# A chunk more ahead of each seven-product down-projection, and the third step of the weight sums by an accumulating DMA

## The chip, the cores and the metric

The kernel runs on one core of a Trainium2 chip, in one launch. The metric is the time of an execution on the device in microseconds (us), the median of several runs. PE is TensorE, DVE VectorE, ACT ScalarE, POOL GpSimd, SP SyncE.

## The reference

Two layers on x of 1024 tokens (8 x 128) and 512 features, all in float32.

```
y  = x W^T + 2 * gated low-rank of 8 experts (top 2)     # _L0_cond_ref
x  = x + series(y) + silu(y Wg^T) * (y Wu^T) Wd^T        # _L0_attn_ref; the FFN has 1248 hidden
z  = x W2^T + b + 2 * LoRA of the sequence's adapter     # _L0_cond2_ref
x  = x + FFN with LoRA (1376 hidden)                     # _L0_ffn_ref
```

The change is in the FFN of the second line (the "first FFN"): 1248 hidden features are padded to 10 chunks of 128.

## The kernel before, in words

Activations lie with features on the partitions. A product in float32 is made as three matmuls of fp32r parts: each operand is split into a high part (ACT copies it, `copy`, L481) and a low part (DVE subtracts, `lo`, L922); low x high, high x low and high x high are summed in PSUM. A matmul here is 128x128 weights on 512 columns.

The first FFN is a series of 14 blocks, `BLOCKS` (L79). A block ("u", c) makes gate and up of chunk c for both halves of the tokens, a block ("d", n) makes a quarter of a down-projection over four chunks. Each is a 2x2 block product made with seven products in place of eight (`seven1`): p1 to p7, each 6 matmuls, 42 per block. The operands of an up block are made once (HT: B11, B21, B22, T1 to T4). Those of a down block are made of the gated chunks: each pair of chunks (even, odd) gives B11 and T1 from the even one, then T2, T3, then B21, B22, then T4 from the odd one, all split, in G. Chunks 8 and 9 (`TAIL`) are not in a down block: they are multiplied in the ordinary way at the end (`tail`, 48 matmuls).

Weights of a block come as two pieces of [128, 512] (`P_BLOCK[q]`, `P_BLOCK[q] + 1`), loaded by SP into a ring of four slots of `raw`, and as `parts`, from which four sums of weights (S1 to S4) are made in three steps: SP loads 1024 columns (L436), POOL adds 768 columns by an accumulating DMA (L462), DVE adds the third summand of two of them (`sums1`, L1089). A region for sums is shared by blocks of one parity. ACT then splits the small part (256 columns, `part1_hi1`) and the large part (1536 columns, `part2_hi1`) for block q + 1 during block q, and DVE makes the low parts (`part1_lo1`, `part2_lo1`). PE may not start block q + 1 before its large low part is there (`ready1`).

The order of work on every engine is written out by hand, as each engine's queue, with semaphores between them. In a usual block PE does p6, p5, p2, p7, p1 of the next block, p3, p4 (`block1`, L1742). DVE: gating of the chunk before (`mul0_1`), its sums (`g_sum`), `sums1`, small low part, low parts of G, `add_b1` (before p3), `add_d1` (before p4), large low part, the second gating (`mul1_1`). ACT: small part, bank copy for C (`copy_bc1`), G's high parts, `copy_e1`, the large part, silu, `copy_ab1` for the next block, silu. Before a down block that follows an up block, PE doesn't take p1 ahead; `enter_down` on PE and ACT has an order of its own, since the last chunk's operands are then only being made.

After the blocks: the tail, x1 = X + down-projection (DVE, L1377), its split, then the second layer's low-rank product (`low_rank2`) and base product (`base`, L1541) with weights W2. ACT and DVE split S13 and S2 (stacks for merging LoRA weights) and W2 after the blocks; SP loads them into the same ring.

Of the kernel before, what the change touches and what calls it, by code (L numbers as in the profile page):

```python
# [14 lines left out]
P = 128  # L15
# [63 lines left out]
BLOCKS = [("u", 0), ("u", 1), ("u", 2), ("u", 3), ("d", 0), ("d", 1), ("u", 4), ("u", 5), ("u", 6), ("u", 7),  # L79
          ("d", 2), ("d", 3), ("u", 8), ("u", 9)]  # L80
# [7 lines left out]
P_BLOCK = []  # L88
for _q in range(len(BLOCKS)):
    P_BLOCK.append(len(SLOT))  # L90
    SLOT += [0, 1] if _q % 2 == 0 else [3, 2]
P_TAIL = len(SLOT)
P_S13 = P_TAIL + 2
P_S2 = P_S13 + 1
P_W2 = P_S2 + 4
SLOT += [0, 1, 2, 3, 0, 1, 2, 3, 0, 1, 2]
# [28 lines left out]
B12 = T4  # L125

# [17 lines left out]
def build(nc, x, ids_b, slot_ids, small, pieces, parts, lora_a, lora_b, stk_up, out):  # L144
    with ExitStack() as ctx:
# [90 lines left out]
        raw_in = [sem(f"raw_in{s}") for s in range(RING)]  # L236
# [80 lines left out]
        def raw_slot(p):  # L317
            k = (0, 1, 6, 7)[SLOT[p]]
            return raw[:, k, :]
# [4 lines left out]
        def before_in_slot(p):  # L324
            return max(q for q in range(p) if SLOT[q] == SLOT[p])
# [60 lines left out]
        def first_down(q):  # L386
            return q <= LAST and not is_up(q) and is_up(q - 1)
# [13 lines left out]

        def event(c, e):
            return 2 * TAIL + 2 * (c - TAIL) + e if c >= TAIL else 4 * (c // 2) + e

        def g_count(c):
            return 2 * TAIL + 2 * (C1 - TAIL) + c + 1
# [8 lines left out]
        def tail_g(c, h):  # L415
            return G[:, 4 * (c - TAIL) + 2 * h + 1]
# [8 lines left out]
        def _(sp):  # L425
# [5 lines left out]
            for p in range(RING, PIECES):  # L431
                if p in P_BLOCK:
                    q = P_BLOCK.index(p)
# [13 lines left out]
        def _(pool):  # L447
# [18 lines left out]
            pool.wait_ge(g_ready, event(TAIL - 1, 3) + 1)  # L466
# [11 lines left out]
        def _(act):  # L478
# [92 lines left out]
            def part1_hi1(q, free, n):  # L571
                act.wait_ge(free, n)
                p = P_BLOCK[q]
# [3 lines left out]
            def part2_hi1(q):  # L577
                p = P_BLOCK[q] + 1
                act.wait_ge(raw_in[SLOT[p]], raw_count(p))
                act.wait_ge(sums_in, q + 1)  # L580
                copy(WU[:, q % 2, 0, PART2[q % 2]], raw_flat[:, RAW2[q % 2]]).then_inc(hi_w, 1)

            def tail_hi(j):
# [4 lines left out]
                copy(tail_w(j)[:, 0, :], raw_slot(p)).then_inc(hi_w, 1)  # L588

# [24 lines left out]
            def g_hi1(c, e=0):  # L614
                if c >= TAIL:
                    act.wait_ge(g_mul[e], c + 1)
                    hi = copy(tail_g(c, e)[:, 0, :], T[:, 2 + e, :])
                elif e == 0:
                    act.wait_ge(g_summed, 3 * (c // 2) + 1)
                    hi = copy(g_ops(c, B11, T1, 0), T[:, 2:7:4, :])  # L620
                elif e == 1:
                    act.wait_ge(g_summed, 3 * (c // 2) + 2)
                    hi = copy(g_ops(c, T2, 1, 0), T[:, 6:8, :])
                elif e == 2:
                    for h in range(HALVES):
                        act.wait_ge(g_mul[h], c + 1)
                    hi = copy(g_ops(c, B21, 1, 0), T[:, 2:4, :])
                else:
                    act.wait_ge(g_summed, 3 * (c // 2) + 3)
                    hi = copy(g_op(c, T4)[:, 0, :], T[:, 2, :])  # L630
                hi.then_inc(hi_g, 1)

            def g_first(q):

                if is_up(q - 1):
                    c = number(q - 1)
                    if c >= TAIL:
                        g_hi1(c, 0)
                        g_hi1(c, 1)
                    else:  # L640
                        g_hi1(c, c % 2)

            def g_later(q, e):
                if is_up(q - 1) and number(q - 1) < TAIL and number(q - 1) % 2:
                    g_hi1(number(q - 1), e)

            def next_a(q):

                if q < LAST and not first_down(q + 1):
                    copy_ab1(q + 1, *b_free(q - 1))  # L650

            def steady1(q):

                part1_hi1(q + 1, p4_done, q)
                copy_bc1(q, *c_free(q - 1))
                g_first(q)
                copy_e1(q)
                g_later(q, 2)
                part2_hi1(q + 1)
                silu1(q, 0)  # L660
                g_later(q, 3)
                next_a(q)
                silu1(q, 1)

            def enter_down(q):

                copy_ab1(q, *b_free(q - 2))
                part1_hi1(q + 1, p4_done, q)
                g_first(q)
                copy_e1(q)  # L670
                g_later(q, 2)
                copy_ab1(q + 1, *b_free(q - 1))
                copy_bc1(q, *c_free(q - 1))
                part2_hi1(q + 1)
                g_later(q, 3)
# [96 lines left out]
            for q in range(1, LAST):  # L772
                (enter_down if first_down(q) else steady1)(q)
            copy_bc1(LAST, *c_free(LAST - 1))
            g_first(LAST)
            copy_e1(LAST)
            tail_hi(0)
            tail_hi(1)
            silu1(LAST, 0)
            silu1(LAST, 1)  # L780
            g_hi1(C1 - 1, 0)
            g_hi1(C1 - 1, 1)


            act.wait_ge(raw_in[SLOT[P_S13]], raw_count(P_S13))
            copy(S13[:], raw_slot(P_S13)[0:KS]).then_inc(hi_w, 1)
            for k in range(4):
                act.wait_ge(raw_in[SLOT[P_S2 + k]], raw_count(P_S2 + k))
                copy(S2[:, k * D:(k + 1) * D], raw_slot(P_S2 + k)[0:KS]).then_inc(hi_w, 1)

            def x1_hi(h):
                act.wait_ge(down1_done, KC * (h + 1))
# [8 lines left out]
            for k in range(KC):  # L801
                w_hi(P_W2 + k, W2[k])
# [108 lines left out]
        def _(dve):  # L911
# [167 lines left out]
            def part1_lo1(q):  # L1079
                dve.wait_ge(hi_w, P_BLOCK[q] + 1)  # L1080
# [3 lines left out]
            def sums1(q):  # L1084
                a = SUM_AT[q % 2]
                two = raw_flat[:, a + 512:a + 1024].rearrange("p (a n) -> p a n", a=2)
                three = raw_flat[:, a + 256:a + 512].unsqueeze(1).to_broadcast([P, 2, 256])
                dve.wait_ge(sum_two[q % 2], 16 * (q // 2 + 1))
                V.tensor_tensor(two, two, three, ALU.add).then_inc(sums_in, 1)  # L1089

            def part2_lo1(q):
                dve.wait_ge(hi_w, P_BLOCK[q] + 2)
# [20 lines left out]
            def mul0_1(c):  # L1113
                dve.wait_ge(p4_done, POS[c] + 1)
                dve.wait_ge(silu[0], c + 1)
                if c:
                    dve.wait_ge(g_ready, event(c - 1, (1 if c > TAIL else 3) if c % 2 == 0 or c > TAIL else 0) + 1)
                V.scalar_tensor_tensor(T[:, 2, :], PB[BANK_C[0]], -1.0, T[:, 0, :], ALU.mult, ALU.mult).then_inc(g_mul[0], 1)

            def mul1_1(c):  # L1120
                dve.wait_ge(added_d, POS[c] + 1)
                dve.wait_ge(silu[1], c + 1)
                if c > TAIL:
                    dve.wait_ge(g_ready, event(c - 1, 1) + 1)
                V.scalar_tensor_tensor(g_home(c, 1), T[:, 5, :], -1.0, T[:, 1, :], ALU.mult, ALU.mult).then_inc(g_mul[1], 1)

            def g_sum(c):

                if c % 2 == 0:
                    dve.wait_ge(g_mul[0], c + 1)  # L1130
# [989 lines left out]
```

## Time and profile before

| | |
|---|---|
| runs | 456.27, 456.35, 457.39 us; median 456.35 |
| profiled execution | 457.57 us, of it the span 455.9 us |
| granted TensorE clock, mean over the span | 0.996 |
| ACT busy | 211.6 us (46%) |
| POOL busy | 29.2 us (6%) |
| DMA | 42.28 MB, mean 93 GB/s |
| first FFN's blocks | 92.6 to 231.1 us of the span |
| tail and first low-rank and base product of layer two | 231.1 to 262.4 us |

The span runs from the first to the last instruction of one profiled execution. Matmuls overlap: each is shown with 0.39 us, but a new one can start every 0.23 us; the distance of starts shows where PE stands. A busy share says how much of the span an engine had an instruction in work.

### The profile page before, as it was taken

The page shows a single profiled execution, that of the slowest core. Times are in us where ns is not written, and L with a number is a line of the kernel's source. Part 1 is how long each engine was busy: PE and PEld are TensorE (multiplying, and loading weights), DVE is VectorE, ACT ScalarE, POOL GpSimd, SP SyncE. Part 2 cuts the span into 40 slices and gives each one's busy share as a digit, 9 for nine tenths or more (in the row PEclk, how much of TensorE's full clock was granted, in tenths as well). Part 3 has the DMA queues.
Part 4 walks back from the last instruction along what each step waited for, and adds up shares of the span by engine and source line. Part 5 has one row for each costly group of instructions (what it writes and reads, how often), then busy time and mean ns, then how long its engine had stood idle before and what let it go on. Part 6 is the DMA issues. An engine that isn't in the chain of part 4 may idle for free.

```text
span 455.9 us, 5562 instructions
## 1 busy us (share of the span) xinstructions
PE 446.5 (98%) x2009; PEld 364.0 (80%) x2009; DVE 324.5 (71%) x471; ACT 211.6 (46%) x324; POOL 29.2 (6%) x51
## 2 busy tenths in 40 slices
PE   8999999999999999999997999999999999999997
PEld 7788888888777888768884888888888888888886
DVE  5755799657987678886568555989963468887731
ACT  6364442355664456553644555556542124565300
POOL 1004100000010100004300000000000000000000
PEclk9999999999999999999999899999999999999999
DMA  8407700136574564637243101222110232112022
GB/s 288 136 0 224 187 1 0 34 94 156 123 197 121 138 155 127 169 89 192 70 128 107 39 0 47 63 58 76 42 47 24 69 92 65 46 47 69 1 93 92
DMA packets 20299, 42.28 MB, mean 93 GB/s; under 512 B 2672, under 2 KB 2944, under 8 KB 20272
## 3 DMA queue, kind: packets, MB, share of 16 engines
q1 hardware_dynamic: 16992, 34.35, 23.4%
q0 software_dynamic: 3280, 7.58, 9.5%
q8 instruction: 16, 0.26, 0.2%
q14 instruction: 11, 0.09, 0.1%
HBM read 39.82 MB, written 2.10 MB: 92 GB/s over the span
## 4 chain that ended last, share of the span: by engine, by line
PE 87%; DVE 8%; ACT 2%; DMA 1%; issue 1%; ACTq 0%; DVEq 0%
PE PS L1676 14%; PE PS L1541 14%; PE PS L1542 14%; PE PS L1543 14%; PE PS L1677 13%; PE PS L1678 13%; DVE G L922 2%; DVE WU L922 1%; DMA raw<-in_pieces 1%; ACT G L481 1%; PE PS L1862 1%; PE PS L1604 1%; DVE X L1377 1%; ACT WU L481 1%; DVE T L1107 1%
## 5 line engine op out<-in xcount | busy, mean ns | idle before, releaser
L1676 PE MATMUL PS<-HT,WU 128*128 128x512 f32 x266 | 103.8, 390 | 0.7 <-DVE WU L922 0.7
L1677 PE MATMUL PS<-HT,WU 128*128 128x512 f32 x266 | 103.6, 390 | 0.0
L1678 PE MATMUL PS<-HT,WU 128*128 128x512 f32 x266 | 103.5, 389 | 0.0
L481 ACT ACTIVATE WU<-raw 128x256 fp32r<-128x256 f32 (+2 forms) x55 | 49.0, 897 | 34.0 <-PE PS L1678 18.1
L922 DVE TENSOR_TENSOR WU<-raw,WU 128x256 fp32r<-128x256 f32 (+2 forms) x56 | 56.5, 1013 | 5.1 <-ACT WU L481 5.0
L1676 PEld LDWEIGHTS PS<-HT,WU 128*128 128x128 f32 x266 | 50.0, 188 | 11.7 <-DVE WU L922 1.5
L481 ACT ACTIVATE PS<-PS 128x512 f32<-128x512 f32 x46 | 26.8, 582 | 68.6 <-PE PS L1678 65.2
L1678 PEld LDWEIGHTS PS<-HT,WU 128*128 128x128 f32 x266 | 49.9, 188 | 10.5
L1677 PEld LDWEIGHTS PS<-HT,WU 128*128 128x128 f32 x266 | 50.0, 188 | 10.1
L922 DVE TENSOR_TENSOR G<-T,G 128x1024 fp32r<-128x1024 f32 (+2 forms) x46 | 43.9, 968 | 18.0 <-ACT G L481 17.1
L481 ACT ACTIVATE G<-T 128x1024 fp32r<-128x1024 f32 (+2 forms) x47 | 39.8, 856 | 20.0 <-DVE T L1038 6.8
L1542 PE MATMUL PS<-G 128*128 128x512 f32 (+1 forms) x102 | 39.4, 386 | 0.0
L1541 PE MATMUL PS<-G 128*128 128x512 f32 (+1 forms) x102 | 39.3, 386 | 0.0
L1543 PE MATMUL PS<-G 128*128 128x512 f32 (+1 forms) x102 | 39.3, 385 | 0.0
L1541 PE MATMUL PS<-G,WU 128*128 128x512 f32 (+1 forms) x99 | 37.9, 383 | 0.0
L1542 PE MATMUL PS<-G,WU 128*128 128x512 f32 (+1 forms) x99 | 37.9, 383 | 0.0
L1543 PE MATMUL PS<-G,WU 128*128 128x512 f32 (+1 forms) x99 | 37.9, 383 | 0.0
L1541 PE MATMUL PS<-HT,G 128*128 128x512 f32 x60 | 24.6, 410 | 3.0 <-DVE X L1377 2.2
L481 ACT ACTIVATE G<-raw 128x512 fp32r<-128x512 f32 (+2 forms) x21 | 12.4, 613 | 26.7 <-PE PS L1543 19.0
L1676 PE MATMUL PS<-G,WU 128*128 128x512 f32 x56 | 22.8, 407 | 1.8 <-DVE WU L922 1.0
L1542 PE MATMUL PS<-HT,G 128*128 128x512 f32 x60 | 24.1, 401 | 0.0
L1543 PE MATMUL PS<-HT,G 128*128 128x512 f32 x60 | 24.0, 399 | 0.0
(170 smaller groups left out, 705.9 us busy)
## 6 DMA issues: line engine op xcount, KB each, us to landing
raw<-in_pieces SPq DMA_DIRECT2D x87, 256.0 KB, 3.7
raw<-in_parts SPq DMA_DIRECT2D x14, 512.0 KB, 3.6
raw<-in_parts POOLq DMA_DIRECT2D x14, 384.0 KB, 4.9
X<-in_x SPq DMA_DIRECT2D x8, 256.0 KB, 5.1
out_x<-X SPq DMA_DIRECT2D x7, 256.0 KB, 2.0
su_raw<-in_stk_up POOLq DMA_DIRECT2D x6, 192.0 KB, 2.7
T<-in_lora_b POOLq DMA_DIRECT2D x16, 32.0 KB, 2.1
ga_raw<-in_lora_a POOLq DMA_DIRECT2D x8, 32.0 KB, 3.4
```

What stands on the lines that cost most here:

```text
L481: return nc.scalar.activation(o, i, ACT.Copy)
L922: return V.tensor_tensor(dst, full, f32(hi), ALU.subtract)
L1107: V.tensor_tensor(T[:, 5, :], PB[BANK_C[0]], T[:, 4, :], ALU.add).then_inc(added_d, 1)
L1377: V.tensor_tensor(X[:, h, c, :], PB[DOWNB[h][c]][:], X[:, h, c, :], ALU.add).then_inc(x1_done, 1)
L1541: pe.matmul(o, w[:, 1, cols], xx[:, 0, :], start=start, stop=False)
L1542: pe.matmul(o, w[:, 0, cols], xx[:, 1, :], start=False, stop=False)
L1543: return pe.matmul(o, w[:, 0, cols], xx[:, 0, :], start=False, stop=stop)
L1604: pe.matmul(PB[LOGITS[1]][:, 0:P], warm[:], warm[:], start=True, stop=True)
L1676: pe.matmul(bank, w[:, 1, cols], hi, start=start and kc == 0, stop=False, skip_group_check=not start)
L1677: pe.matmul(bank, w[:, 0, cols], low, start=False, stop=False, skip_group_check=not start)
L1678: mm = pe.matmul(bank, w[:, 0, cols], hi, start=False, stop=kc == 1, skip_group_check=not start)
L1862: mm = pe.matmul(bank, S13[:, chunk(d)], SU[:, c % 2 * 2 * P:(c % 2 + 1) * 2 * P], start=True, stop=True)
```

## The change

Four things. (1) The order of blocks: u4 before d0 and u8 before d2. PE's and ACT's `enter_down` go; all blocks from 1 on run in the usual order on PE (`block1`), which now takes p1 of the next block ahead everywhere. (2) The third step of the sums: `sums1` on DVE goes; POOL waits for its first DMA and issues a second accumulating one, SBUF to SBUF, which adds a region of 256 columns to two others. Of the first piece, SP loads only the 256 columns that are used, and ahead of the sums. (3) The ring of `raw` gets two more slots after the last even block's sums. (4) Block 13 has its own order, `last`: S13, S2, the tail's weights and W2 are split in blocks 12 and 13. In the down blocks, DVE's first addition to X stands behind the large low part. x1's low parts are interleaved with its additions, and ACT doesn't wait for a whole half.

```diff
-BLOCKS = [("u", 0), ("u", 1), ("u", 2), ("u", 3), ("d", 0), ("d", 1), ("u", 4), ("u", 5), ("u", 6), ("u", 7),
-          ("d", 2), ("d", 3), ("u", 8), ("u", 9)]
+BLOCKS = [("u", 0), ("u", 1), ("u", 2), ("u", 3), ("u", 4), ("d", 0), ("d", 1), ("u", 5), ("u", 6), ("u", 7),
+          ("u", 8), ("d", 2), ("d", 3), ("u", 9)]
...
-SLOT += [0, 1, 2, 3, 0, 1, 2, 3, 0, 1, 2]
+SLOT += [0, 1, 4, 5, 3, 2, 0, 1, 4, 5, 3]
...
@@ SP, in the loop over the pieces
+                k, q = BLOCK_PIECES[p - P_FFN] if P_FFN <= p < P_S13 else (None, None)
+                if k == 1:
                     if q > 1:
-                        sp.wait_ge(w_ready, P_BLOCK[q - 2] + 2)
+                        sp.wait_ge(w_ready, P_TWO[q - 2] + 1)
                     sp.dma_start(sum_region(q), parts[q][:, 0:1024]).then_inc(sum_in[q % 2], 16)
                 sp.wait_ge(w_ready, before_in_slot(p) + 1)
-                sp.dma_start(raw_slot(p), pieces[p]).then_inc(raw_in[SLOT[p]], 16)
+                if k == 0:
+                    a11 = slice(256 * (q % 2), 256 * (q % 2) + 256)
+                    sp.dma_start(raw_slot(p)[:, a11], pieces[p][:, a11]).then_inc(raw_in[SLOT[p]], 16)
+                else:
+                    sp.dma_start(raw_slot(p), pieces[p]).then_inc(raw_in[SLOT[p]], 16)
@@ POOL, sums_by_dma
                 pool.dma_start(raw_flat[:, at:at + 768], parts[q][:, 1024:1792], accum_op=ALU.add).then_inc(sum_two[k], 16)
+                pool.wait_ge(sum_two[k], 16 * n)
+                pool.dma_start(raw_flat[:, at + 512:at + 1024].rearrange("p (a n) -> p a n", a=2),
+                               raw_flat[:, at + 256:at + 512].unsqueeze(1).to_broadcast([P, 2, 256]),
+                               accum_op=ALU.add).then_inc(sums_in, 16)
@@ ACT, new or changed
             def steady1(q):
+                c = number(q - 1) if is_up(q - 1) else None
+                odd = c is not None and c % 2 == 1
                 part1_hi1(q + 1, p4_done, q)
                 copy_bc1(q, *c_free(q - 1))
+                if odd:
+                    two_hi(c, ("T2", "T3"), (T2, 1), T[:, 6:8, :])
+                elif c is not None and is_up(q):
+                    two_hi(c, ("T1",), (B11, T1), T[:, 2:7:4, :])
                 copy_e1(q)
+                if odd:
+                    b2_hi(c)
                 part2_hi1(q + 1)
+                if second_down(q):
+                    ...
                 silu1(q, 0)
+                if odd:
+                    t4_hi(c)
+                if q == LAST - 1:
+                    s13_hi()
+                    s2_hi(0)
+                copy_ab1(q + 1, *b_free(q - 1))
                 silu1(q, 1)
+            def last(q):
+                s2_hi(1)
+                copy_bc1(q, *c_free(q - 1))
+                s2_hi(2)
+                copy_e1(q)
+                s2_hi(3)
+                tail_hi(0)
+                tail_hi(1)
+                silu1(q, 0)
+                for k in range(2):
+                    w_hi(P_W2 + k, W2[k])
+                silu1(q, 1)
+                for h in range(HALVES):
+                    tail_g_hi(C1 - 1, h)
+                for k in range(2, KC):
+                    w_hi(P_W2 + k, W2[k])
@@ DVE
-            def sums1(q):
-                ...
-                V.tensor_tensor(two, two, three, ALU.add).then_inc(sums_in, 1)
+            def steady1(q):
+                c = number(q - 1) if is_up(q - 1) else None
+                odd = c is not None and c % 2 == 1
+                if c is None:
+                    x_out(q - 1, "c")
+                else:
+                    mul0_1(c)
+                    if odd:
+                        t2_t3_sums(c)
+                    elif c < TAIL:
+                        t1_sum(c)
+                part1_lo1(q + 1)
+                if odd:
+                    two_lo(c, "T2", (T2, 1), T[:, 6:8, :])
+                elif c is not None and is_up(q):
+                    two_lo(c, "T1", (B11, T1), T[:, 2:7:4, :])
+                add_b1(q)
+                if odd:
+                    two_lo(c, "B21", (B21, 1), T[:, 2:4, :])
+                    t4_sum(c)
+                add_d1(q)
+                part2_lo1(q + 1)
+                if odd:
+                    t4_lo(c)
+                if second_down(q):
+                    ...
+                if is_up(q):
+                    mul1_1(number(q))
+                else:
+                    x_out(q, "a")
+                    x_out(q, "d")
+                    x_out(q, "b")
+                if q == LAST - 1:
+                    s13_lo()
+                    s2_lo(0)
+            def last(q):
+                x_out(q - 1, "c")
+                s2_lo(1)
+                s2_lo(2)
+                add_b1(q)
+                s2_lo(3)
+                tail_lo(0)
+                tail_lo(1)
+                add_d1(q)
+                for k in range(2):
+                    w_lo(P_W2 + k, W2[k])
+                mul1_1(C1 - 1)
+                mul0_1(C1 - 1)
+                for h in range(HALVES):
+                    tail_g_lo(C1 - 1, h)
+                for k in range(2, KC):
+                    w_lo(P_W2 + k, W2[k])
...
             def x1(h):
+                x1_add(h, 0)
+                for c in range(1, KC):
+                    x1_add(h, c)
+                    x1_lo(h, c - 1)
+                x1_lo(h, KC - 1)
@@ PE
-                if q < LAST and not first_down(q + 1):
+                if q < LAST:
                     p1_1(q + 1, *a_free(q - 1))
...
-            def enter_down(q):
-                ...
-                (enter_down if first_down(q) else block1)(q)
+                block1(q)
```

## Rows read from the trace of the kernel before

**Rows 1.** The page, busy time, share of the span, instructions: PE and DVE.
```profile
PE 446.5 (98%) x2009; PEld 364.0 (80%) x2009; DVE 324.5 (71%) x471; ACT 211.6 (46%) x324; POOL 29.2 (6%) x51
```

**Rows 2.** Waits of PE: waiting line, releaser, us in total, times, longest.
```profile
PE PS L1541 <- DVE X L1377: 2.2, 1, 2.2
PE PS L1676 <- DVE WU L922: 1.6, 4, 0.5
...
PE PS L1676 <- DVE T L1107: 0.8, 2, 0.4
```

**Rows 3.** Timeline of PE, chosen starts: start us, us, engine, line, operation.
```profile
92.59 0.39 PE L1676 MATMUL PS<-HT,WU 128*128 128x512 f32 x1
...
122.28 0.39 PE L1678 MATMUL PS<-HT,WU 128*128 128x512 f32 x1
123.01 0.50 PE L1676 MATMUL PS<-HT,WU 128*128 128x512 f32 x1 [0.34 <-DVE WU L922]
...
133.80 0.39 PE L1678 MATMUL PS<-G,WU 128*128 128x512 f32 x1
134.66 0.50 PE L1676 MATMUL PS<-G,WU 128*128 128x512 f32 x1 [0.47 <-DVE WU L922]
...
141.55 0.39 PE L1678 MATMUL PS<-G,WU 128*128 128x512 f32 x1
142.36 0.50 PE L1676 MATMUL PS<-G,WU 128*128 128x512 f32 x1 [0.42 <-DVE T L1107]
...
231.14 0.39 PE L1541 MATMUL PS<-G,WU 128*128 128x512 f32 x1
...
262.44 0.39 PE L1910 MATMUL PS<-HT,G 128*128 128x512 f32 x1
```

**Rows 4.** The pause before 250.04, and the stretch behind it (third last column: PEclk).
```profile
250.04 0.50 PE L1541 MATMUL PS<-HT,G 128*128 128x512 f32 x1 [2.19 <-DVE X L1377]
...
250.80:254.20 3.40, 3.40 (x9) 2.63 (x8) 3.38 (x6) 3.40 (x5) 0.00 (x0) 0.50 0.19 69
```

**Rows 5.** Timeline of ACT and DVE in block 2 (behind chunk 1).
```profile
117.50 1.48 ACT L481 ACTIVATE WU<-raw 128x1536 fp32r<-128x1536 f32 x1
...
120.59 0.69 DVE L922 TENSOR_TENSOR G<-T,G 128x512 fp32r<-128x512 f32 x1
121.20 1.75 DVE L922 TENSOR_TENSOR WU<-raw,WU 128x1536 fp32r<-128x1536 f32 x1
```

**Rows 6.** Line L1089 (`sums1`): count, duration ns min/median/max, first and last start.
```profile
L1089 DVE TENSOR_TENSOR raw<-raw x14: 677/683/687, 84.7 to 214.3; 128x512 f32<-128x512 f32 x14
```

**Rows 7.** DMA issues (us to landing); then L462's and L470's times to landing.
```profile
raw<-in_pieces SPq DMA_DIRECT2D x87, 256.0 KB, 3.7
raw<-in_parts SPq DMA_DIRECT2D x14, 512.0 KB, 3.6
...
DMA to landing us min/median/max: 4.7/4.9/8.0
...
DMA to landing us min/median/max: 1.9/2.1/3.6
```

**Rows 8.** Timeline of SP's queue: the first step of the sums, block 2's end.
```profile
122.98 0.33 SPq L436 DMA_DIRECT2D raw<-in_parts  x1
```

**Rows 9.** Timeline of DVE in the second down block (block 5).
```profile
149.79 0.69 DVE L1107 TENSOR_TENSOR T<-PS,T 128x512 f32<-128x512 f32 x1 [0.67 <-PE PS L1678]
150.40 1.75 DVE L922 TENSOR_TENSOR WU<-raw,WU 128x1536 fp32r<-128x1536 f32 x1
152.07 0.68 DVE L1167 TENSOR_TENSOR X<-X,T 128x512 f32<-128x512 f32 x1
```

**Rows 10.** Timeline of ACT: a bank copy behind an addition to X; four copies for S.
```profile
145.80 0.58 ACT L481 ACTIVATE PS<-PS 128x512 f32<-128x512 f32 x1 [1.33 <-DVE X L1167]
...
233.12 2.18 ACT L481 ACTIVATE S<-raw 96x512 fp32r<-96x512 f32 x4
```

More of the change, by code:

```diff
@@ L87 @@
 SLOT = [p % RING for p in range(P_FFN)]
-P_BLOCK = []
+P_ONE, P_TWO, BLOCK_PIECES = {}, {}, []
 for _q in range(len(BLOCKS)):
[L90 to L93, printed above, removed]
+    for _n in range(2):
+        (P_ONE, P_TWO)[_n][_q] = len(SLOT)
+        BLOCK_PIECES.append((_n, _q))
+        SLOT.append(((0, 1), (3, 2))[_q % 2][_n])
+P_S13 = len(SLOT)
 P_S2 = P_S13 + 1
-P_W2 = P_S2 + 4
-SLOT += [0, 1, 2, 3, 0, 1, 2, 3, 0, 1, 2]
+P_TAIL = P_S2 + 4
+P_W2 = P_TAIL + 2
+SLOT += [0, 1, 4, 5, 3, 2, 0, 1, 4, 5, 3]
 P_CHUNK, P_HALF, P_FULL = [], 0, 0
@@ L125 @@
 B12 = T4
+G_SUM, G_SPLIT = {}, {}
+for _c in range(0, TAIL, 2):
+    G_SUM[_c, "T1"] = 3 * _c // 2 + 1
+    G_SPLIT[_c, "T1"] = 2 * _c + 1
+    for _n, _names in enumerate((("T2", "T3"), ("T4",))):
+        for _name in _names:
+            G_SUM[_c + 1, _name] = 3 * _c // 2 + 2 + _n
+    for _n, _names in enumerate((("T2", "T3"), ("B21", "B22"), ("T4",))):
+        for _name in _names:
+            G_SPLIT[_c + 1, _name] = 2 * _c + 2 + _n
+for _c in range(TAIL, C1):
+    for _h in range(2):
+        G_SPLIT[_c, _h] = max(G_SPLIT.values()) + 1
+G_SPLITS = max(G_SPLIT.values())
 BANK_A, BANK_B, BANK_C, BANK_E = ((2, 4), (0, 2)), ((3, 5), (1, 3)), (1, 5), (0, 4)
@@ L384, in number, with second_down @@
             return BLOCKS[q][1]
-        def first_down(q):
-            return q <= LAST and not is_up(q) and is_up(q - 1)
+        def second_down(q):
+            return not is_up(q) and not is_up(q - 1)
         def a_free(q):
@@ L633, in g_first, with tail_g_hi @@
[L633 to L647, printed above, removed]
-                if q < LAST and not first_down(q + 1):
-                    copy_ab1(q + 1, *b_free(q - 1))
+            def tail_g_hi(c, h):
+                act.wait_ge(g_mul[h], c + 1)
+                copy(tail_g(c, h)[:, 0, :], T[:, 2 + h, :]).then_inc(hi_g, 1)
@@ new lines, in two_hi, with b2_hi, t4_hi @@
+            def two_hi(c, names, at, src):
+                act.wait_ge(g_summed, G_SUM[c, names[0]])
+                copy(g_ops(c, *at, 0), src).then_inc(hi_g, 1)
+            def b2_hi(c):
+                for h in range(HALVES):
+                    act.wait_ge(g_mul[h], c + 1)
+                copy(g_ops(c, B21, 1, 0), T[:, 2:4, :]).then_inc(hi_g, 1)
+            def t4_hi(c):
+                act.wait_ge(g_summed, G_SUM[c, "T4"])
+                copy(g_op(c, T4)[:, 0, :], T[:, 2, :]).then_inc(hi_g, 1)
@@ L772, in _ @@
             for q in range(1, LAST):
[L773 to L789, printed above, removed]
+                steady1(q)
+            last(LAST)
             def x1_hi(h):
-                act.wait_ge(down1_done, KC * (h + 1))
                 for c in range(KC):
@@ L1334, in _ @@
             t_lo(T3, T[:, 6:8, :], 4)
-            sums1(0)
             part1_lo1(0)
@@ L2046, in first_ffn @@
         up_piece, down = ffn(a["L0_attn_ffn_gate_w"], a["L0_attn_ffn_up_w"], a["L0_attn_ffn_down_w"], C1)
-        got, parts = [], []
+        blocks, parts = [], []
         for q, (what, c) in enumerate(BLOCKS):
@@ L2054, in first_ffn @@
                                        for j in rows[k]], axis=1) for k in range(2)]
-            got += two
+            blocks.append(two)
             (a11, a21), (a12, a22) = ([t[:, :256], t[:, 256:]][::-1 if q % 2 else 1] for t in two)
             parts.append(np.concatenate([a21, a11, a12, a22, a22, a21, a22], axis=1))
-        return got + list(down[TAIL:]), parts
+        return [blocks[q][n] for n, q in BLOCK_PIECES], list(down[TAIL:]), parts
     def second_ffn():
@@ L2076 @@
               [a13] + [padded(wide(a2[:, k:k + D]), 32) for k in range(0, C2 * P, D)] + [padded(a["L0_ffn_lora_B2"].T, 32)]]
-    firsts, parts = first_ffn()
-    pieces += firsts + [padded(w, P) for w in stacks] + list(by_chunk(a["L0_cond2_W"]).transpose(1, 0, 2))
+    firsts, tail, parts = first_ffn()
+    pieces += firsts + [padded(w, P) for w in stacks] + tail + list(by_chunk(a["L0_cond2_W"]).transpose(1, 0, 2))
     pieces += second_ffn()
```

239 lines of the change are left out of this document (76 added, 163 removed).

## The prediction

> **What bounds the kernel now.** Read the page's busy part first. PE is busy for 446.5 us of a span of 455.9, DVE for 324.5 [rows 1]. So time can only come from the few places where PE stands still or runs slowly. The waits of PE say who makes it stand: after the start, only DVE, in single pieces of 0.4 to 2.2 us [rows 2]. The timeline of PE gives their places [rows 3]. Block 0 has 48 matmuls and every later block 42, so from 92.59 (first matmul of block 0) to 122.28 (last of block 2) there are 131 steps, 0.2267 us each, without a gap. I use this pitch as the floor. The 14 blocks hold 588 matmuls, 133.3 us at that pitch; the trace takes 231.14 - 92.59 = 138.55. So 5.25 us are lost in the blocks, all around the two entries into the down-projection. The pairs of neighbours in [rows 3] show the first entry: 0.73 between starts at 122.28, 0.86 at 133.80, 0.81 at 141.55, and a few smaller ones that I leave to the 5.25; the second entry, from 182 us, repeats them.
>
> From 231.14 (first matmul of the tail) to 262.44 (first of the second low-rank product) I count 48 tail, 8 low-rank, 48 base and 8 added low-rank matmuls: 112, or 25.4 us at the floor. The trace takes 31.3, so 5.9 us are lost. The largest piece is a pause before 250.04: 2.19 idle, PE waiting for the addition into X [rows 4]. Right behind it, from 250.8 to 254.2, the granted clock is 0.50 (the 1.2 GHz level of the two): 9 matmuls in 3.4 us, where the floor is about 2.0. The whole reserve is thus 5.25 + 5.9 = 11.15 us.
>
> **The change, part by part.**
>
> *Order of blocks; "enter_down" goes.* Before, down block 4 follows up block 3, whose chunk is still to be gated, summed and split, and block 4's first product waits for that: this is the 0.86 at 133.80 and what follows. After, up block u4 (u8) stands between, with six products while T2, T3, B21, B22 and T4 are made; T1 is made a block earlier still. No matmul is added. What is late next is DVE's work in the block behind an odd chunk, which already costs the 0.73 at 122.28: PE waits for the last weights' low part, which runs from 121.20 for 1.75 us, to 122.95 [rows 5]. PE could have used it at 122.28 + 0.23 = 122.51. The change puts the split of T4 (starting 120.59, 0.61 before the next start) behind this operation, so it begins at 120.59 and ends at 122.35; without the DVE sum (0.68, next paragraph) it can be earlier only as far as ACT's copies allow, so I count nothing for that. 122.35 is 0.15 before 122.51. All four entries' stalls go: -5.25. If this margin fails, 0.1 to 0.6 us come back in each of four such blocks.
>
> *Third step of the sums by DMA.* 14 DVE additions of 0.683 go [rows 6], 9.6 us of DVE. DVE is not PE's bound outside those blocks, so nothing is counted for them. In their place POOL waits for the second step, issues an addition from SBUF into SBUF (128 partitions, two pieces of 1 KB, 256 KB in all), and ACT's copy of the large weight part waits for it. Before, nothing like it is in the trace. The nearest rows: the 32 KB plain DMAs of POOL land in 2.1 us, the 384 KB accumulating ones in 4.9 (4.7 to 8.0) [rows 7]. A 256 KB accumulation lies between; I take 4.9, the same kind of operation, since its pieces are a third as long but twice as many. Is it hidden? The first load of the sums for block q+1 is issued when the low part for q-1 is done: 122.98, 0.03 after 122.95 [rows 5, 8], with the new order 0.6 earlier, at 122.38. Block 2 starts at 122.51 - 9.52 = 112.99, so that is 9.4 after the start of a block behind an odd chunk, and 9.6 before the start of the like block two further on, where ACT copies these sums. Add 3.6 (first step [rows 7]), 0.3 to POOL's issue, 4.9, 4.9 and 0.1: landing 4.2 after its start. ACT begins this copy at 117.50, 4.5 after it [rows 5]. It is hidden, with 0.3 to ACT's turn. In blocks behind an even chunk DVE has fewer operations ahead of the low part, so the issue is earlier, and ACT fewer copies ahead of its turn, so the turn is too; I take the same. If it is later, ACT slips first, PE only when the loop is full: 3.6 + 0.3 + 4.9 + L + 0.2, then ACT 1.48 and DVE 1.75, in two blocks of 9.52. That gives L = 6.8 us; above this each us costs 0.5 per block. Half of the first piece's load (its unused 128 KB) goes, which frees some DMA time: 0.
>
> *x_out after the last weights in a down block.* Before, X's first addition of a down block sat in an idle gap of DVE; now it stands after the large low part, and in block 12 two splits of the tail's operand, then three additions to X, the low parts of S13 and S2's first quarter, and the fourth addition stand in one queue. The trace's second down block shows the start of this queue: the large low part begins at 150.40, right behind an addition at 149.79 that waited for PE's fourth product, and the next operation at 152.07 [rows 9]. The fourth product ends 5.45 after a block's start (24 matmuls), DVE starts 0.04 later, so the queue starts 152.07 - 149.79 + 5.49 = 7.77 after block 12's start. Eight operations at 0.60 (0.61 from 120.59 to 121.20, and 149.79 to 150.40 [rows 5, 9]) end at 12.6, which is 3.1 after block 13's start. Only then may ACT copy bank C (0.03 later, 0.58 long [rows 10]): 3.7, before PE's fourth product at 4.08. But in block 13 ACT copies S2's third quarter next (four take 2.18, so some 0.52 apiece [rows 10]), to 4.25, and DVE waits for it: it starts that low part at 4.28, add_b at 4.88, S2's last at 5.48, two tail weights at 6.08 and 6.68, add_d at 7.28, and ends that at 7.97. PE's last product needs add_d and would start 6.81 after the block's start. It starts at 8.03. That is a new wait of 1.2, and 0.1 to refill: +1.3. Its bounds: 0 (if ACT and DVE catch up) and 2.0 (if the second tail weight, loaded only when S13 is split at about 1.9, lands after 5.7: a piece takes 3.7 [rows 7]).
>
> *The tail.* The splits of W2 move from behind X's half 0 to block 13, and each low part of X follows its addition by one. DVE's old queue put S2's last quarter and four W2 splits, with two waits on loads, ahead of the second half's additions: this made the pause before 250.04. New queue of DVE, worked out with the same 0.60, from block 13's start: weights 0 and 1 at 7.9, gating and its splits to 12.2, weights 2 and 3 to 13.4, two LoRA splits to 14.1, X half 0 (eight at 0.6, and 0.3 of waits) to 19.2. PE's tail starts at 9.5 and ends at 20.4: low-rank finds all four parts. The second half's additions end before the base product comes to their banks. So the stalls and, with no pause, the slow stretch go: -5.9. Bounds: 0 and -5.9.
>
> The Trainium skill (SBUF — State Buffer, "The DMA setup-cost knee") puts a transfer at about 2 us plus its bytes over 436 GB/s. That would make L about 2.6 us, an estimate from that page; the 384 KB rows' 4.9 is longer than its 2.9, so the measurement decides, and by either the sum is the same.
>
> **Sum.** 5.25 + 5.9 - 1.3 = 9.85 us off. The profiled execution took 457.57 (span 455.9, 1.7 around it), so its like would be 447.7. It ran 1.2 above the median of the three runs, 456.35; from that, 446.5. A little may stay of the many small waits: I say 446.7.
>
> **Rivals.**
> (A) The entries' stalls only move: DVE stays late in the blocks behind odd chunks (margin 0.15), or ACT's turn slips. For it: DVE is back to back there [rows 5]. Against: 0.6 us is taken out just there. Only the tail's gain less 1.3 is left: 456.35 - 4.6 = 451.7; a half of it, 449.2.
> (B) The tail's pause stays in part, because a load of W2 in a slot freed only in block 13 comes late. For: such loads made ACT wait before (the pause before 250.04 came behind them). Then 5.25 less 1.3: 452.4.
> (C) Slower: the third step is late. Place: ACT's large copy in every block. It decides from L = 6.8; at 0.5 us per block and us over 12 blocks, 6 us per us, the gain is eaten at L = 6.8 + 9.85 / 6 = 8.4. At L = 10 the time would be 446.5 + 19.2 = 465.7. For it: the longest accumulating DMA took 8.0 [rows 7], and the first step of the next sums (512 KB) is issued just when this one moves. Against: that 8.0 is one of 14, median 4.9. The Trainium skill (SBUF — State Buffer, "SBUF: two separate sides") knows such a delay: DVE in a two-port mode keeps GpSimd from writing descriptors. Here POOL's accumulating DMAs land in 4.7 or 4.9 beside a busy DVE, so it does not show.
> (D) The new wait in block 13 does not come: 445.4.
>
> **Chances.** Forecast with D 0.74 (445.2 to 447.8), A 0.11, B 0.07, C 0.05 slower and 0.01 even, something else even 0.02. Range 445.2 to 450.0: it holds the forecast and half of A. A measurement of this kernel tells 0.3% (1.4 us) from no change: faster 0.92, same 0.03, slower 0.05.
>
> **What would show it.** Right: in PE's starts the blocks run at 0.2267 without gaps of 0.7 or more until the last, where the last product waits some 1.2 us for DVE's add_d; no pause before the base product, and granted clock 1.00 there. ACT's large copy waits for no DMA. Wrong: PE waiting for WU at the starts of blocks; ACT waiting for raw; a third step above 6.8 us; a stretch at clock 0.50.

## The result, and the profile after

The changed kernel takes 451.65 us (median of four runs, 450.98 to 452.84), the kernel before 456.31 beside it (four runs). The ratio is 0.990, interval 0.9867 to 0.9934: faster by 1%. The prediction was 446.7, range 445.2 to 450.0. The sign was right, the size was not: half of the gain that was worked out is missing. Measured once more beside other runs (e11 below), the changed kernel came out at 451.14 against 457.00 (ratio 0.9889, interval 0.9864 to 0.9914), so the miss is not an accident of one measurement.

The profiled execution took 452.84 us, its span is 450.9. The first line of its page answers to [rows 1], the three lines under them are its DMA issues (KB each, us to landing) and answer to [rows 7].

```profile
PE 443.5 (98%) x2009; PEld 364.2 (81%) x2009; DVE 316.6 (70%) x457; ACT 211.6 (47%) x324; POOL 46.4 (10%) x65
...
raw<-in_parts SPq DMA_DIRECT2D x14, 512.0 KB, 4.0
raw<-in_parts POOLq DMA_DIRECT2D x14, 384.0 KB, 5.2
raw<-raw POOLq DMA_DIRECT2D x14, 256.0 KB, 5.9
```

DVE has 14 instructions and 7.9 us less, POOL 17 us more. PE's busy time moved by 3.0 us only, since PE has the same 2009 matmuls in both. The third step (raw<-raw) lands 5.9 us after its issue (median), where 4.9 was put in; the first step takes 4.0 in place of 3.6, the second 5.2 in place of 4.9.

The timeline of PE, chosen starts, answers to [rows 3] and [rows 4]. The first of them is the first of block 0, the last two are the first of the tail and of the second low-rank product.

```profile
93.11 0.39 PE L1691 MATMUL PS<-HT,WU 128*128 128x512 f32 x1
...
180.53 0.50 PE L1691 MATMUL PS<-HT,WU 128*128 128x512 f32 x1
190.87 0.50 PE L1691 MATMUL PS<-HT,WU 128*128 128x512 f32 x1 [0.53 <-DVE WU L942]
221.10 0.47 PE L1691 MATMUL PS<-HT,WU 128*128 128x512 f32 x1 [1.26 <-ACT PS L507]
225.90 0.50 PE L1691 MATMUL PS<-HT,WU 128*128 128x512 f32 x1 [0.46 <-ACT PS L507]
227.88 0.50 PE L1691 MATMUL PS<-HT,WU 128*128 128x512 f32 x1 [0.32 <-DVE PS L1116]
230.52 0.50 PE L1691 MATMUL PS<-HT,WU 128*128 128x512 f32 x1 [1.00 <-DVE T L1120]
...
232.01 0.40 PE L1556 MATMUL PS<-G,WU 128*128 128x512 f32 x1
...
257.46 0.39 PE L1916 MATMUL PS<-HT,G 128*128 128x512 f32 x1
```

Read it with the same floor of 0.2267 per matmul. The 112 matmuls from 232.01 to 257.46 take 25.45, the floor is 25.4: the tail's 5.9 us are gone entirely, as forecast. The 588 of the blocks take 232.01 - 93.11 = 138.90, the floor is 133.3: 5.6 us are lost, more than the 5.25 before. But they lie elsewhere. All gaps at the entries into the down-projection are gone. There are 1.2 us at 180.53 and 190.87 (starts of blocks, a gap and the 0.1 to refill), and 4.1 us in block 13, from 221.10 to 230.85, where 1.3 were forecast (small distances make up the rest).

The stretches of the tail (us, busy times, then the granted clock, DMA share, GB/s) show no pause and no slow clock; the second answers to the last row of [rows 4].

```profile
242.90:257.40 14.50, 14.50 (x65) 11.77 (x64) 7.31 (x11) 6.96 (x11) 0.53 (x1) 1.00 0.05 15
246.00:249.40 3.40, 3.40 (x17) 2.81 (x16) 2.80 (x4) 2.83 (x4) 0.00 (x0) 1.00 0.00 0
```

Who is late in the blocks? The waits of ACT (waiting line, releaser, us in total, times, longest), a view in which raw<-raw can't have stood before:

```profile
ACT WU L507 <- DMA raw<-raw: 21.6, 11, 3.2
```

ACT's large copy waited for the third step 11 times out of 14. This was a sign named for "wrong". Three places of the timelines of POOL, SP and ACT show when:

```profile
96.40 1.19 POOL L486 DMA_DIRECT2D raw<-raw  x1 [4.26 <-DMA raw<-in_parts]
...
111.63 1.20 POOL L486 DMA_DIRECT2D raw<-raw  x1 [4.39 <-DMA raw<-in_parts]
112.01 0.33 SPq L454 DMA_DIRECT2D raw<-in_parts  x1
112.39 0.43 SPq L460 DMA_DIRECT2D raw<-in_pieces  x1
118.49 1.49 ACT L507 ACTIVATE WU<-raw 128x1536 fp32r<-128x1536 f32 x1 [0.36 <-DMA raw<-raw]
...
141.89 0.33 SPq L454 DMA_DIRECT2D raw<-in_parts  x1
142.27 0.43 SPq L460 DMA_DIRECT2D raw<-in_pieces  x1
142.29 1.20 POOL L486 DMA_DIRECT2D raw<-raw  x1 [4.83 <-DMA raw<-in_parts]
```

The third step issued at 111.63 released ACT at 118.49, 6.9 us later. SP issued 768 KB of loads for another block's weights 0.4 and 0.8 us behind it. The one at 142.29 stands 0.4 us behind such loads and landed after 5.6. The one issued at 96.40 had no such company and landed after 4.1; the shortest of the 14 took 3.8. Ten third steps, from 111.63 to 200.27, have loads issued within 0.7 us of them: the four that were issued ahead of the loads took 6.3 to 6.9, the six issued behind the first of them 5.4 to 6.6. To be first did not make them faster.

And the end, in the timelines of ACT and DVE:

```profile
216.91 1.49 ACT L507 ACTIVATE WU<-raw 128x1536 fp32r<-128x1536 f32 x1 [3.17 <-DMA raw<-raw]
...
220.38 0.57 ACT L507 ACTIVATE PS<-PS 128x512 f32<-128x512 f32 x1
...
225.26 0.58 ACT L507 ACTIVATE PS<-PS 128x512 f32<-128x512 f32 x1 [3.76 <-DVE X L1177]
...
218.43 1.76 DVE L942 TENSOR_TENSOR WU<-raw,WU 128x1536 fp32r<-128x1536 f32 x1 [1.94 <-ACT WU L507]
...
224.54 0.69 DVE L1177 TENSOR_TENSOR X<-X,PS 128x512 f32<-128x512 f32 x1
...
229.78 0.69 DVE L1120 TENSOR_TENSOR T<-PS,T 128x512 f32<-128x512 f32 x1
```

In block 12 the large copy waits 3.17 us. Its third step, issued at 211.05, landed after 5.8, and the second step ahead of it after 6.2. Behind the large copy on ACT stand four copies and then the bank copy for block 13, at 220.38, for which PE stands 1.26 us (221.10). On DVE the large low part starts 1.94 us late, and the whole queue of the prediction follows it: fourth addition to X at 224.54, bank copy of C at 225.26 (PE 225.90), add_b (PE 227.88), add_d at 229.78 (PE 230.52).

### The profile page after: what moved, and what is told of

Same layout as the page of the kernel before. It is cut to its first block, busy times and chain, and to the rows that moved or that the text cites. A ratio compares the mean times of both kernels' runs of the same rounds, so it can differ in the third digit from the quotient of the medians.

```text
span 450.9 us, 5568 instructions
## 1 busy us (share of the span) xinstructions
PE 443.5 (98%) x2009; PEld 364.2 (81%) x2009; DVE 316.6 (70%) x457; ACT 211.6 (47%) x324; POOL 46.4 (10%) x65
## 4 chain that ended last, share of the span: by engine, by line
PE 72%; DMA 16%; DVE 6%; issue 2%; ACT 2%; POOL 0%; ACTq 0%; DVEq 0%; POOLq 0%
PE PS L1556 15%; PE PS L1557 15%; PE PS L1558 15%; DMA raw<-in_parts 9%; PE PS L1691 8%; PE PS L1692 8%; PE PS L1693 8%; DMA raw<-raw 7%; DVE WU L942 3%; ACT WU L507 2%; PE PS L1868 1%; PE PS L1619 1%; DVE G L942 1%; DVE X L1177 1%; DVE T L1120 0%
## 5 line engine op out<-in xcount | busy, mean ns | idle before, releaser
L942 DVE TENSOR_TENSOR HT<-HF,HT 128x512 fp32r<-128x512 f32 (+1 forms) x15 | 14.1, 939 | 14.3 <-ACT HF L838 12.6
L1556 PE MATMUL PS<-HT,G 128*128 128x512 f32 x60 | 24.0, 400 | 0.0
L486 POOL DMA_DIRECT2D raw<-raw x14 | 16.8, 1201 | 67.7 <-DMA raw<-in_parts 67.7
L1557 PE MATMUL PS<-HT,G 128*128 128x512 f32 x60 | 23.7, 394 | 0.0
L1558 PE MATMUL PS<-HT,G 128*128 128x512 f32 x60 | 23.5, 392 | 0.0
```

The lines of the kernel that those rows point to most:

```text
L486: pool.dma_start(raw_flat[:, at + 512:at + 1024].rearrange("p (a n) -> p a n", a=2), raw_flat[:, at + 256:at + 512].unsqueeze(1).to_broadc ...
L942: return V.tensor_tensor(dst, full, f32(hi), ALU.subtract)
L1556: pe.matmul(o, w[:, 1, cols], xx[:, 0, :], start=start, stop=False)
L1557: pe.matmul(o, w[:, 0, cols], xx[:, 1, :], start=False, stop=False)
L1558: return pe.matmul(o, w[:, 0, cols], xx[:, 0, :], start=False, stop=stop)
```

## The experiments

Four theories were open: the third step is late by what runs beside it; it is late by its own make; block 13's order costs by itself; and the time taken off DVE was the gain. All times below are medians, and the ratios are to runs of the kernel before on the same chip, which took 455 to 458 us.

**e1_sum_on_dve.** The changed kernel with the third step back on DVE.

```diff
-                pool.wait_ge(sum_two[k], 16 * n)
-                pool.dma_start(<two sums>, <third summand>, accum_op=ALU.add).then_inc(sums_in, 16)
+            def sums1(q):  # as before, ahead of part1_lo1(q + 1)
```

> The changed kernel with only the third step of the weight sums put back on DVE (14 additions of 0.68 us, as before); order of blocks, last block and tail stay changed. Theory 1 (the third step by DMA comes late because it meets the next loads of the sums; the loop load, second step, third step, ACT's copy, DVE's low part is full at two blocks, and this also starts the queue of blocks 12 and 13 some 2 us late): ACT's large copy waits for no DMA, the 1.2 us lost before block 13 go, and of the 4.4 us lost in block 13 about 1.3 stay; 451.65 falls to 447 to 448. Theory 2 (the late third step costs only the 1.2, block 13's loss is its own order of work): 450 to 450.5. Theory 3 (DVE's 0.6 us per block were the gain in blocks 2, 4, 8, 10): 453 or more, with PE waiting for DVE WU at block starts.

Measured 448.71 us (448.48 to 449.38), ratio to before 0.9803 (0.9784 to 0.9821). ACT has no wait for a DMA in the blocks. The waits of PE that are left, but for one at the program's start:

```profile
PE PS L1697 <- DVE T L1123: 1.0, 1, 1.0
PE PS L1697 <- DVE PS L1119: 0.3, 1, 0.3
```

No gap before block 13, and there 2.0 us in place of 4.1: add_d (p4) 1.15 and 0.1 to refill, add_b (p3) 0.5 and 0.1, and 0.2. Theory 1 holds: the late third step costs 3.3 us in the traces, 1.2 at starts of blocks and 2.1 in block 13, and 2.4 to 2.9 between the medians (451.14 or 451.65 against 448.71, not measured side by side). The time is 0.7 above the upper end that theory 1 gave: block 13 kept 2.0 us, where about 1.3 was expected.

**e2_order.** The third step stays by DMA; in the down blocks and block 13 the queues of DVE and ACT are ordered anew.

```diff
@@ DVE, a block
+                if not is_up(q): x_out(q, "a")
+                if q == LAST - 1: tail_g_lo(TAIL, 0); tail_g_lo(TAIL, 1)
                 add_d1(q)
+                if not is_up(q): x_out(q, "d")
                 part2_lo1(q + 1)
...
-                    x_out(q, "a")
-                    x_out(q, "d")
                     x_out(q, "b")
@@ DVE, last
                 x_out(q - 1, "c")
+                s2_lo(0)
@@ ACT: tail_g_hi ahead of part2_hi1, copy_ab1 ahead of s13_hi and s2_hi(0)
```

> The changed kernel with the third step still by DMA, but another order of work in the down blocks and block 13: two of the additions to X before the large low part, the fourth addition ahead of S2's splits, the tail operand's splits before add_d, and on ACT the bank copy for block 13 ahead of S13 and S2. Theory 1: the third step still lands 6 us after its issue, ACT still waits for it, the 1.2 us before block 13 stay; block 13 loses at most 1 us instead of 4.4: 448 to 449. Theory 2: the same or better, 447.5 to 448.5. If the order was not the cause: 451 to 452.

Measured 448.87 us (447.55 to 451.92), ratio 0.9817 (0.9787 to 0.9847). ACT's line is now

```profile
ACT WU L507 <- DMA raw<-raw: 15.5, 10, 3.1
```

so the third step is still late, and PE still stands at starts of blocks (0.5 and 0.1 at 170.89, 0.1 and 0.1 at 180.63 and at 209.41), but block 13 loses 0.4. Either cure alone gives nearly the same, 2.9 and 2.8 us off 451.65. The spread differs: 0.9 us over five runs with the sum on DVE, 4.4 over six with the DMA, so a single run of e2 says less.

**e3_both.** Both edits together.

> Both: third step on DVE and the other order of work. Theory 1 and 2: nothing is lost in the blocks, 446 to 447, and PE's starts keep 0.2267 us from block 0 to the tail. If the two causes are one (the order matters only when the third step is late): the same as with the third step on DVE alone.

Measured 446.90 us (446.80 to 447.21), ratio 0.9767 (0.9749 to 0.9786). In the stretch of the blocks PE has one gap above 0.1, in block 13 (0.3 and 0.1), and no wait but the one at the program's start:

```profile
PE PS L1626 <- DVE warm L1000: 1.1, 1, 1.1
```

Its blocks take 226.23 - 92.53 = 133.70, 0.4 above the floor. This is the version that beats both kernels, 2.3% under the one before, and it comes out at the time that the prediction gave to the change, though not by the same sum (see below).

**e4_before_dma.** The kernel before with only the third step by DMA (the pair of lines of e1, the other way).

> The kernel before with only the third step of the sums moved from DVE to the accumulating DMA. Theory 1: the loop is full there too, so ACT waits for the third step, PE loses more in the blocks than before, but the two entries into the down-projection hide a part: 457 to 459. If the third step by DMA were harmless, DVE's 0.6 us would shorten the 0.73 at the block behind an odd chunk: 455 to 456.

Measured 458.98 us (456.41 to 461.79, 12 runs), ratio 1.004 (1.0015 to 1.0064): slower, little. The part alone costs; it is not paid by DVE's 0.68 us. The profiled execution was the fastest of the 12, 456.41, so what the slower ones lose was not seen. In this profile the third step's time to landing (min/median/max) is

```profile
DMA to landing us min/median/max: 3.8/4.1/7.5
```

The 7.5 belongs to the one issued at 111.09, 0.3 us ahead of the next loads (111.39). Those with no load issued within 1.9 us of them took 3.8 to 4.7. With the stalls at the entries left in, most third steps stand clear of the loads here, hence the median of 4.1.

**e5_small_loads.** What runs beside the third step is taken away: from block 2 on only 64 of 1024 columns of the first step are loaded, and 64 of 512 of the second piece. The rest of these weights is left out, so this kernel doesn't compute the reference.

```diff
+                    n = 64 if q > 1 else 1024
-                    sp.dma_start(sum_region(q), parts[q][:, 0:1024])
+                    sp.dma_start(sum_region(q)[:, 0:n], parts[q][:, 0:n])
```

> The changed kernel with the loads beside the third step made small: from block 2 on SP loads 64 of the 1024 columns of the first step and 64 of the 512 columns of the second piece; the rest of these weights is not loaded (the output is not the reference's), all instructions stay. Theory 1 (the third step takes 6 to 7 us because its packets share the DMA engines with the next block's loads): issue to landing falls to 4.0 to 4.5 us, as in block 2's where no load ran beside it; ACT's large copy waits for no DMA; time 448 to 449, as with the sum on DVE. Theory 2 (its own 256 pieces of 1 KB, and SBUF to SBUF, make it long): 5.5 us and more stays, ACT still waits 1 to 3 us, though the first step is shorter, and the time is 450 or more.

Measured 449.92 us (448.82 to 450.57). The third step (same 256 pieces of 1 KB, SBUF to SBUF):

```profile
DMA to landing us min/median/max: 3.8/3.9/5.2
```

ACT doesn't wait for it, the blocks before 13 have no gap, block 13 loses 2.1. Two of them (issued at 130.12 and 187.62) still stand 0.6 and 0.2 us ahead of the small loads and landed after 4.0 and 3.8. So it is the size of the loads beside it, not the moment of issue: 2.0 of the 5.9 us come from sharing with them. The time is 0.9 above the range expected; the profiled run (448.82) is in it, and what the slower runs lose was not seen.

**e6_third_from_hbm.** Other pieces: 128 of 2 KB from HBM in place of 256 of 1 KB from SBUF. It adds another matrix than the reference's.

```diff
-                pool.dma_start(<two sums of 256>, <one region, twice>, accum_op=ALU.add)
+                pool.dma_start(raw_flat[:, at + 512:at + 1024], parts[q][:, 1792:2304], accum_op=ALU.add)
```

> The changed kernel with the third step's summand read from HBM as 128 pieces of 2 KB in place of 256 pieces of 1 KB from SBUF (it adds another matrix, so the output is not the reference's). Theory 1 (sharing the DMA engines): still 5 to 6.5 us to landing, ACT still waits, 450 to 452. Theory 2 (number and size of the pieces): 4 to 4.9 us, 448 to 449.5.

Measured 451.91 us (450.27 to 452.79). The third step and ACT's wait for it:

```profile
DMA to landing us min/median/max: 4.1/5.9/7.1
...
ACT WU L506 <- DMA raw<-in_parts: 20.8, 10, 3.7
```

The same 5.9. Number, size and source were changed together, so that one made up for the other isn't excluded by this run alone; but e5 kept all three and landed in 3.9. The two together leave the sharing as the cause of the 2.0 us.

**e8_t4_first.** From e3: T4's split back ahead of the large low part on DVE (`t4_lo(c)` ahead of `part2_lo1(q + 1)`).

> The same version (446.9 us), with T4's split back ahead of the large low part on DVE. Theory 1 (DVE is late by 0.5 to 0.6 us in the blocks behind an odd chunk, and the split's place alone cures it): PE waits 0.5 to 0.7 us for DVE WU at the start of blocks 3, 5, 9 and 11, 2.4 us in all: 448.5 to 449.5. Theory 2 (the slack is larger than 0.6): 447, no gap.

Measured 449.76 us (449.40 to 450.14), against 446.9. PE stands at the start of blocks 3, 5, 9 and 11, each with 0.73 or 0.74 from start to start and 0.33 or 0.34 behind, 2.5 us in all above the floor:

```profile
PE PS L1698 <- DVE WU L937: 1.4, 4, 0.3
```

This is the step of the prediction with a margin of 0.15 us, and it is right: the place of one split of 0.6 us is worth 2.5 us in the trace and 2.9 in the time.

**e7_old_tail.** From e3: the work behind block 13 put back (W2's splits behind X's half 0, low parts behind all additions, ACT waiting for a whole half).

> The version with the sum on DVE and the other order of work (446.9 us), with only the work behind block 13 put back: W2's splits behind X's half 0, X's low parts behind all four additions, ACT waiting for a whole half. Theory 1 (this order made the pause before the base product): PE stands 3 us or more at the start of the base product, with a stretch at clock 0.50 behind it if the pause exceeds 2 us: 450 to 453. Theory 2 (the late loads of W2 and of S2's last quarter made it, and the new ring slots cured that): 447 to 448.5.

Measured 446.84 us (446.76 to 447.53): no difference. The tail takes 25.43 us, as in the changed kernel. Theory 1 is refuted; the prediction had given this order, with its waits on loads, as the cause of the pause.

**e10_s2_early.** The kernel before, with one instruction of DVE moved.

```diff
-            for k in range(3):
+            for k in range(4):
                 s2_lo(k)
...
             x1(0)
-            s2_lo(3)
```

> The kernel before with one instruction of DVE moved: the low part of S2's last quarter ahead of X's half 0 instead of behind it (it frees the slot into which the last quarter of W2 is loaded). Theory 1 (the pause before the base product came from that late load): the load lands 5 us earlier, the pause of 2.2 us goes, and the stretch at clock 0.50 behind it too, 2.3 to 4 us less than before: 453 to 455. Theory 2 (the pause came from DVE's four W2 splits standing ahead of the second half's additions): at most 1 us less, 456 to 457.5.

Measured 453.58 us (453.12 to 454.16), beside 457.00; ratio 0.9934 (0.9914 to 0.9954). The chain that made the pause, in timelines of the kernel before (DVE, SP, ACT, DVE):

```profile
244.06 0.68 DVE L1369 TENSOR_TENSOR S<-raw,S 32x512 fp32r<-32x512 f32 x1
244.77 0.33 SPq L438 DMA_DIRECT2D raw<-in_pieces  x1
248.03 0.63 ACT L481 ACTIVATE G<-raw 128x512 fp32r<-128x512 f32 x1 [4.18 <-DMA raw<-in_pieces]
248.69 0.69 DVE L922 TENSOR_TENSOR G<-raw,G 128x512 fp32r<-128x512 f32 x1 [2.02 <-ACT G L481]
249.30 0.68 DVE L1377 TENSOR_TENSOR X<-PS,X 128x512 f32<-128x512 f32 x1
```

S2's last quarter is split at 244.06 and frees the slot; W2's last quarter is loaded into it at 244.77 and lands 3.3 us later; its split holds up the addition to X for which PE stands. With the split moved, ACT copies all four quarters in one go, DVE's four follow, and PE's start is at 247.15, with 0.46 from start to start (timelines of ACT, DVE, PE of e10):

```profile
242.25 2.18 ACT L481 ACTIVATE G<-raw 128x512 fp32r<-128x512 f32 x4
...
244.01 2.49 DVE L922 TENSOR_TENSOR G<-raw,G 128x512 fp32r<-128x512 f32 x4
...
247.15 0.50 PE L1540 MATMUL PS<-HT,G 128*128 128x512 f32 x1
```

Theory 1 of this run holds: the load made the pause, and a single moved instruction gives 3.4 us between the medians, with the clock at 1.00 behind it. From the tail's first matmul to the second low-rank product the trace has 26.88 us in place of 31.3, 4.4 less; the profiled execution of the kernel before is one with the slow stretch.

**e9_sp_order.** The changed kernel, with SP issuing the first step ahead of the first piece, as before.

> The changed kernel with one thing put back: on SP the first step of the sums is again issued ahead of the block's first piece, so that all three loads of a block go together, instead of the first piece (128 KB) about 6 us earlier, where the second step runs. If that early piece is what makes the second step longer (5.2 us against 4.9) and so pushes the third into the next loads: second step 4.9 or less, third step under 5 us in most blocks, ACT's waits for it halved, 449 to 450. If the third step meets the first step's load whatever the piece does: 451 to 452, third step 5.5 to 6 us.

Measured 452.22 us (448.77 to 453.80), and the third step:

```profile
DMA to landing us min/median/max: 3.8/4.9/7.0
```

Inconclusive. In the profiled run (the 449.98 of the six) the second step is at 4.9 and ACT's waits fell from 14.2 us (the changed kernel on the same chip) to 9.3, as the first theory has it, but the median is 1 us above e11's, not below. That the early first piece costs time is neither shown nor excluded.

**e11_changed_again.** The changed kernel on that chip.

> The changed kernel once more, beside the two others on the same chip: 451 to 452.5, third step 5.5 to 6.2 us, ACT's large copy waits for it in ten blocks or more. If its time were a matter of the chip, it would come out under 450 or above 453.

Measured 451.14 us (450.22 to 452.84). Third step 5.4 us, ACT waits in nine blocks: both a little less than expected, the time as expected.

## Why the prediction was wrong, by its steps

*Floor and reserve (11.15 us).* Right. e3 comes within 0.4 us of the floor in the blocks, and its profiled execution took 446.83, which is 457.57 - 11.15 + 0.4.

*The start of the sum.* Probably about 1 us too low. From the profiled 457.57 the sum gave 447.7; the forecast took it from the median of 456.35 instead. But part of the tail's 5.9 us is the slow stretch, and an execution that doesn't have it can't gain it: beside e1 the kernel before has spans of 456.0 us at a mean clock of 0.996, that of the trace with the stretch, and of 454.3 at 1.000 (medians). To which kind 456.27 and 456.35 belong isn't known. That e3 matches 446.7 is thus in part luck: it loses 0.4 in the blocks where the sum has 1.3.

*Entries, -5.25, by the new order and T4's place.* Right. No entry shows a gap, and e8 shows that T4's place carries about 2.5 us, by the mechanism given, with the gap of 0.73 that [rows 3] have.

*Tail, -5.9.* Right in size (25.45 against 31.3), wrong in cause. The prediction blamed DVE's queue: S2's last quarter and four W2 splits, with two waits on loads, ahead of the second half's additions. e7 has the W2 splits there and no pause. What goes in the change is the load of W2's last quarter behind a slot that S2's split freed too late (e10: 4.4 us of the 5.9 by the traces). That the right size came from another cause is luck; the change happened to remove both.

*Third step, 0.* This step failed. It called the third step hidden, with L = 4.9 from a row of another operation, which in the blocks of the kernel before was issued about 4 us or more ahead of the next loads. In the changed kernel the issue falls within 0.7 us of them, and L is 5.9 (3.9 with the loads made small, e5). The prediction named this company under rival C and priced it as if only L above 6.8 would count. But the loop holds all three steps: with the measured medians it is 4.0 + 0.3 + 5.2 + 5.9 + 0.2 + 1.49 + 1.76 = 18.85 of 19.04 us. It is full at an L of 6.1, not 6.8, and single blocks are over it (up to 6.9). The shift also feeds itself: when the third step is late, the large low part is late, and the loads that wait for it are issued later. PE loses 1.2 us directly.

*Block 13, +1.3.* Right in its mechanism, even in its last number (add_d 1.15), but mis-sized: 4.1 in the profile, 2.0 when the third step is on time (e1). Of the 0.7 between 1.3 and 2.0, 0.6 is p3's wait for add_b with its refill, which isn't in the sum. The working let block 12's queue start at 7.77 by [rows 9], where the large low part waited for nothing. With the third step late it waits 1.94 us, and everything behind it moves, PE's waits too; and on ACT it brings a wait that wasn't in the sum at all, the bank copy for block 13 (1.26 us).

Together: 5.25 + 5.9 - 5.6 = 5.55 off the profiled 457.57 gives 452.0, measured 452.84 (0.5 of the rest lies ahead of block 0: 93.11 against 92.59). The blocks lost 4.3 more than the sum had: 3.3 by the late third step, 0.7 by block 13's own order, the rest in small distances. The start of the sum adds about 1 to the miss of 5.0 between the medians.

*Rivals.* C was the right mechanism with a chance of 0.06 and only its even and slower ends written down; its mild form was given to no case. A had the right time (451.7) for another reason, and so, nearly, had B (452.4): that is luck of the number, since neither the entries nor the tail kept a stall.

## What to carry to other kernels

A transfer put between two transfers of a ring is not hidden because it fits ahead of its reader; add up the whole loop from the freed slot back to the freed slot, with the longest times that rows show for steps that run beside other transfers, and take what is left as the margin. Work out as well when each step is issued against the next loads. Where a queue begins with an operation that waits on such a loop, its lateness moves all that is behind, so a better order of the queue after it (e2) was worth as much here as the loop's cure (e1). And before a pause is put down to the instructions ahead of the late one, follow the longest wait in that queue to its load and to who freed the slot: that was one instruction's place.

## What the runs showed of the hardware

An accumulating DMA of 256 KB from SBUF into SBUF lands after about 4 us with no large load issued near it (4.1 at 96.40 in the changed kernel, 3.8 to 4.0 in ten of the last twelve of e5, up to 4.7 in e4), and after 5.4 to 6.9 in the changed kernel where 512 KB and 256 KB of loads are issued within 0.7 us of it. Issued up to 0.7 us ahead of them it took 6.3 to 6.9, issued behind the first of them 5.4 to 6.6; so an earlier issue did not put it ahead. POOL is occupied 1.20 us with its 256 pieces, 0.86 with 128 (e6). The Trainium skill (SBUF — State Buffer, "The DMA setup-cost knee") would have 256 KB at about 2.6 us, an estimate; no such DMA of any run here got below 3.8.

The kernel before has runs with a mean granted clock of 0.996 and runs with 1.000. Beside e1 there were 11 of the one kind, with spans of 455.3 to 456.7 us, 5 of the other, with 453.8 to 455.3, and one at 0.999. The one trace at 0.996 has the stretch at the 1.2 GHz level behind the pause of 2.2 us [rows 4]. If that stretch is what makes 0.996 in the others too, which was not looked at, it follows the pause in most executions, not in all, and costs some 1.7 us (an estimate, from medians of 456.0 and 454.3). The profiled execution of e4 has a pause of 1.8 us at the same place and a clock of 1.00 behind it. None of the six runs of e10, with the pause gone, is below 1.000.

The spread differs between the versions: 0.4 to 0.9 us over five runs each of e1, e3, e7 and e8, which have the third sum on DVE, against 1.8 to 5.0 where it is a DMA (1.9 and 2.6 for the changed kernel, 1.8 in e5, 2.5 in e6, 4.4 in e2, 5.0 in e9). In e5 no copy of the profiled run waits for the DMA, so the full loop alone doesn't explain the spread; what else does is open.
